# The borders of two layers in a two-layer attention and mixture-of-experts kernel: other orders on five engines, and key tiles with three maxima units in layer 0

## The reference: what is computed

```
x = x + L0_xattn(layernorm(x), ctx)      # 8 heads of 4
x = x + L0_ffn(layernorm(x))             # 8 experts, top 2, capacity 640
x = x + L1_xattn(layernorm(x), ctx)      # 16 heads of 16
x = x + L1_ffn(layernorm(x))             # 15 experts, top 3, and a shared one
# attention: softmax(q k^T * scale) v per head, then a projection with bias
```

## Time and profile before

| | us |
|---|---|
| median of 3 runs | 1242.67 |
| lowest, highest | 1241.54, 1252.23 |
| time of the profiled execution | 1248.94 |
| its span | 1247.2 |
| PE busy | 1107.5 (89%) |
| DVE busy | 751.6 (60%) |
| ACT busy | 527.8 (42%) |
| POOL busy | 474.8 (38%) |
| mean granted TensorE clock | 0.929 |

### The profile page before, as it was taken

How to read it: one execution, slowest core, us unless ns; L and a number is a source line. 1 busy time by engine, 2 the same in 40 slices (tenths; PEclk the granted TensorE clock), 3 DMA queues, 4 the chain that set the end, 5 groups by cost and what they waited for, 6 DMA issues and landing times. The chain is left out here.

```text
span 1247.2 us, 20458 instructions
## 1 busy us (share of the span) xinstructions
PE 1107.5 (89%) x6708; PEld 761.6 (61%) x6709; DVE 751.6 (60%) x1466; ACT 527.8 (42%) x1074; POOL 474.8 (38%) x518
## 2 busy tenths in 40 slices
PE   4788877699999999999658899998878999999997
PEld 1244444599999999999523444454545455555554
DVE  6878668367458557643467887876067244444427
ACT  4266653345336335522326666666324122323210
POOL 4203430556356546421335354102014066656510
PEclk9599987799999999999859999989568999999999
DMA  5122213533133123120343132320381422222242
GB/s 176 28 93 93 78 46 98 194 127 111 52 117 127 61 83 128 53 96 18 102 111 116 57 104 87 103 87 2 127 303 53 167 72 72 77 80 77 56 168 102
DMA packets 68048, 121.63 MB, mean 98 GB/s; under 512 B 16993, under 2 KB 36232, under 8 KB 67206
## 3 DMA queue, kind: packets, MB, share of 16 engines
q1 hardware_dynamic: 57894, 96.28, 23.6%
q0 software_dynamic: 10080, 24.38, 6.1%
HBM read 89.84 MB, written 33.82 MB: 99 GB/s over the span
## 5 line engine op out<-in xcount | busy, mean ns | idle before, releaser
L739 ACT ACTIVATE PT<-S 128x512 f32<-128x512 f32 x384 | 203.8, 599 | 124.3 <-PE S L717 123.3
L754 DVE TENSOR_REDUCE M<-S 128x2 f32<-128x1024 f32 x192 | 225.2, 1219 | 34.4 <-PE S L693 33.9
L510 PE MATMUL bankm<-XSTh,w12h 128*128 128x320 f32 x512 | 163.2, 319 | 5.3 <-DVE HF L594 5.2
L510 PE MATMUL bankm<-XSTl,w12h 128*128 128x320 f32 x512 | 159.7, 312 | 0.0
L510 PE MATMUL bankm<-XSTh,w12l 128*128 128x320 f32 x512 | 159.6, 312 | 0.0
L693 PE MATMUL S<-KS,QS 62*128 62x512 f32 x384 | 92.6, 498 | 43.2 <-DVE M L754 18.0
L588 DVE TENSOR_TENSOR HTl<-HF,HTh 128x320 fp32r<-128x320 f32 x128 | 129.7, 1013 | 1.0
L2199 PE MATMUL bank<-W,XST 128*128 x248 | 121.0, 610 | 4.6 <-issue 1.3
L717 PE MATMUL S<-QS,KS 64*128 64x512 f32 x384 | 112.0, 491 | 5.9 <-DMA QS<-NM 5.2
L727 PE MATMUL PV<-PT,VA 128*32 128x256 f32 x1536 | 109.6, 406 | 3.7 <-ACT PT L739 2.4
L554 ACT ACTIVATE SG<-bankm 128x320 f32<-128x320 f32 x128 | 56.1, 438 | 117.0 <-PE bankm L510 115.9
(11 more groups left out here) (274 smaller groups left out, 2008.6 us busy)
## 6 DMA issues: line engine op xcount, KB each, us to landing
stage<-in_W12T SPq DMA_DIRECT2D x32, 512.0 KB
stage<-in_W3T SPq DMA_DIRECT2D x16, 512.0 KB
W<-in_fc1T SPq DMA_DIRECT2D x2, 3840.0 KB, 18.8
YG<-yk SPq DMA_DIRECT2D x4, 1536.0 KB, 12.4
yk<-zeros SPq DMA_DIRECT2D x4, 1024.0 KB, 4.7
KS<-scrk SPq DMA_DIRECT2D x32, 128.0 KB, 2.7
scrq<-parts SPq DMA_DIRECT2D x16, 256.0 KB
QS<-scrq SPq DMA_DIRECT2D x30, 128.0 KB, 2.5
```

Of the source, the lines that this page charges most:

```text
L510: m = pe.matmul(bank[:, c % 2, 0:HALF], ew.w12[a][s][:, k, f:f + P], XST[b][:, k, half * HALF:(half + 1) * HALF], start=(k == 0 and (a, b) ...
L739: act.activation(self.PT[:, kt, 2 * j + h, :], self.S2[:, n % 3, :], ACT.Exp, scale=self.lay.scale).then_inc(self.exp_done, 1)
L754: dve.tensor_reduce(self.M[:, g % 2, :, h, q], got, AX.X, ALU.max).then_inc(self.ring.dve_free, 1)
```

## The change

Layer 0:
- FRONT0 falls from 14 to 10. The first scores come after unit (1,1), and key tiles 0 to 3 have three units each.
- DVE's `first_stats(3)` moves from ahead of `keep_values(1)` to behind the negation of group 0's maxima.

Layer 1:
- PE makes 11 value tiles ahead of the queries, and the other 5 between units (0,1) to (0,5). The bias products move behind the turn of group 0's maxima. XN of batch 1 is turned in key tile 2 instead of 0.
- ACT writes the ones of KS slots 0 and 1 after the eighth value copy, slot 2 after the twelfth, slot 3 after the last.
- DVE copies into QS ahead of the low part of query 1; the statistics of batch 1 move behind the negation of group 0's maxima.
- POOL clears QS slots 1 and 2 right after the ones in VA, and slot 3 after all value tiles.
- SP stores both queries ahead of the queries of group 1, and waits for slot 3's zeros and ones ahead of the loop.

```
-FRONT0, FRONT1 = AHEAD, UNITS + 2
+FRONT0, FRONT1, EARLY = UNITS + 2, UNITS + 2, 11
-TURN_XN, QUERY = {(0, 0): 1, (0, 15): 2, (1, 15): 3}, ...
+TURN_XN, QUERY = {(0, 2): 1, (0, 15): 2, (1, 15): 3}, ...
...
             low_keys(1)
-            first_stats(3)
             keep_values(1)
...
             at.negate(dve, 0)
+            first_stats(3)
...
+            at.load(sp, 1, "k")
+            store(0, 0)
+            store(0, 1)
+            sp.wait_ge(zeros_done, 1)
+            load(1, "q")
             sp.wait_ge(ones_done, 2)
-            at.load(sp, 1, "k")
-            sp.wait_ge(zeros_done, 1)
-            store(0, 0)
-            load(1, "q")
-            store(0, 1)
...
+            sp.wait_ge(zeros_done, 2)
+            sp.wait_ge(ones_done, 3)
             for g in range(NG):
...
+            pool.memset(at.QS[:, 1:SLOTS - 1, :, :].bitcast(F32), 0.0).then_inc(zeros_done, 1)
             pool.wait_ge(v_ready, NT)
-            pool.memset(at.QS[:, 1:, :, :].bitcast(F32), 0.0).then_inc(zeros_done, 1)
+            pool.memset(at.QS[:, SLOTS - 1, :, :].bitcast(F32), 0.0).then_inc(zeros_done, 1)
...
-            for t in range(NT):
+            for t in range(EARLY):
                 value(t)
...
-            pe.wait_ge(v_done, NT)
+            pe.wait_ge(v_done, EARLY)
...
             for u in range(UNITS):
                 at.maxima(pe, 0, u)
+                if 1 <= u <= NT - EARLY:
+                    value(EARLY + u - 1)
+            at.maxima(pe, 1, 0)
+            at.turn(pe, 0)
             pe.wait_ge(wo_loaded, 32)
...
-            at.maxima(pe, 1, 0)
-            at.turn(pe, 0)
...
-            for t in range(NT):
+            for t in range(EARLY):
                 keep_value(t)
-            fill_keys(slice(0, 1), 1)
+                if t == 2 * TPB - 1:
+                    fill_keys(slice(0, 2), 2)
...
-            fill_keys(slice(1, SLOTS), SLOTS - 1)
+            for t in range(EARLY, NT):
+                keep_value(t)
+                if t == 3 * TPB - 1:
+                    fill_keys(slice(2, 3), 1)
+            fill_keys(slice(3, 4), 1)
...
             low(0, 0)
-            low(0, 1)
             dve.wait_ge(at.picked, 2)
             dve.tensor_copy(at.QS[:, 0, 1, :], at.S2[:, 1, :]).then_inc(at.dve_stack, 1)
-            dve.wait_ge(added, 2 * PER)
-            link(norm_tiles(dve, pre, X, range(TPB, 2 * TPB)))
-            norm_seed(dve, link, pre, 1)
+            low(0, 1)
...
             at.negate(dve, 0)
+            dve.wait_ge(added, 2 * PER)
+            link(norm_tiles(dve, pre, X, range(TPB, 2 * TPB)))
+            norm_seed(dve, link, pre, 1)
```

More of the change, by code:

```diff
@@ L784 @@
 GPB1 = 16 // GH
-FRONT0, FRONT1 = AHEAD, UNITS + 2
+FRONT0, FRONT1, EARLY = UNITS + 2, UNITS + 2, 11
 TURN_OT, PROJECT, TURN_XF, ROUTE = 3, (4, 7), 11, 12
-TURN_XN, QUERY = {(0, 0): 1, (0, 15): 2, (1, 15): 3}, {(0, 3): (1, 0), (0, 4): (1, 1), (1, 0): (2, 0), (1, 8): (2, 1),
+TURN_XN, QUERY = {(0, 2): 1, (0, 15): 2, (1, 15): 3}, {(0, 3): (1, 0), (0, 4): (1, 1), (1, 0): (2, 0), (1, 8): (2, 1),
                                                        (2, 0): (3, 0), (2, 8): (3, 1)}
@@ L842, in ring0 @@
     names += [("max", 0, u) for u in range(UNITS)] + [("max", 1, 0), ("turn", 0)]
-    names += [("max", 1, u) for u in range(1, AHEAD - UNITS)]
+    names += [("max", 1, u) for u in range(1, FRONT0 - UNITS)]
     for g in range(NG):
```

## The result

| | before | changed |
|---|---|---|
| median of 20 runs, us | 1248.64 | 1242.09 |
| lowest, highest | 1239.84, 1254.34 | 1228.74, 1250.84 |
| ratio to before | | 0.9941, 95% interval 0.9917 to 0.9965 |
| profiled execution | 1248.94 | 1245.86 |

The change makes the kernel faster by 0.59% (0.35 to 0.83%), 7.4 us of 1248.64. The forecast was 12.2 us and 1230.5. So the forecast missed the changed kernel's median by 11.6: 6.0 in the starting point and 5.6 in the difference of the medians (6.55 instead of 12.2).

A forecast was written before the change was run, and what follows sets the result against it. The prediction took a single chain at each layer's start, up to the first scores, as the bound. Layer 1's -11.3 and layer 0's -0.9 made -12.2, from the median 1242.67 to 1230.5 us; range 1224.5 to 1239.5.

The forecast's parts named there:

- Steps 1 and 2: Layer 1 start: five value tiles leave the path, -4.3; KS fill moved, -0.4; POOL's clear of QS delays XN, +0.8.
- Step 3: Layer 1 start: copy into QS ahead of query 1's low part, batch 1 statistics moved, so reductions begin earlier; -2.65 us.
- Step 4: Layer 1 start: five value tiles between units make PE the bound there, +0.7 us, if the clock is 2.4 GHz.
- first rival: Layer 1's five value tiles between units run at 1.2 GHz: 5.9 us more than step 4, 1236.4; chance 12%.
- Steps 5 and 6: Layer 1 start: bias products run during NM's transfer, -2.0; NM's shift no longer waits in SP's queue, -2.95.
- Step 7: Layer 1 key tiles: XN's turn leaves key tile 0, -1.9, and goes to key tile 2 at 2.4 GHz; -0.5 net.
- the halving's wait: Layer 1, key tile 1: halving meets POOL's bias additions, longer by up to about 0.4 us; left out of the sum.
- third rival: Starts gain and key tiles give it back; layer 0 loses 2 to 4 us, or XN is late: 1236 to 1240; 11%.
- the case for a slower kernel: Clock fails to rise in layer 0's DVE-bound key tiles, each costing 2.07 us more at 1.2 GHz: 1255; chance 4%.

The follow-up runs named there:

- layer 1's part alone: Kernel before with only the layer 1 edits, FRONT0 and the place of the statistics as before; 1238.42 to 1243.33 before, ratio 0.9975.
- statistics in key tile 0: Changed kernel with FRONT0 back at 14 and layer 0's statistics of batch 3 moved into key tile 0; 1236.42 to 1243.33 before, ratio 0.9942.
- products at key tiles 17 to 20: Changed kernel with four unread 256-column products on PE, one at each of those key tiles of layer 0; 1236.54 to 1244.05 before, ratio 0.995.
- the later bias additions: Changed kernel with POOL's bias addition of layer 1's first two row tiles done one group later; 1237.46 to 1244.05 before, ratio 0.995.

## Why the prediction was wrong, step by step

The terms below are means over the profiles of kernels with the same code in the stage. Layer 1 as before: 4 profiles. Layer 1 as changed: 6 (both of the changed kernel, layer 1's part alone, statistics in key tile 0, products at key tiles 17 to 20, and the later bias additions, whose edit is worth at most 0.8 there). Layer 0 as before: 3. Layer 0 as changed: 7.

| | forecast | measured |
|---|---|---|
| L1, to first scores | -10.8 | 36.4 - 47.0 = -10.5 |
| L1, key tiles 0 to 3 | -0.5 | 22.5 - 21.3 = +1.2 |
| L1, all to the last exponential | -11.3 | 282.4 - 292.0 = -9.6 |
| L0, to first scores | -5.8 | 41.2 - 46.3 = -5.1 |
| L0, key tiles 0 to 3 | +4.95 | 23.5 - 17.3 = +6.2 |
| L0, all to the first value tile | -0.9 | 603.6 - 601.3 = +2.3 |
| sum | -12.2 | -7.3 |

The sum of the stages, -7.3, fits the -7.4 of the run times, closer than it had to. Single profiles of one code scatter by 7 us in the row of layer 1's whole attention and by 8 in that of layer 0, so the two wholes are good to some 3 us each. The rows to the first scores and of the key tiles scatter by 1 to 4. The scatter of layer 1's whole lies in its last eight key tiles: without them the gain is 10.0 where the row has 9.6.

*The number* is where it went most wrong: the step that failed is the last, "I carry the difference over to the median". With the median of the 20 runs, 1248.64, the same difference gives 1236.4. I noted that the profiled execution was 6.3 above the median of three, "with nothing in these stretches that would explain it". What explains it lay in stretches that I had not read. The second profile of the same kernel took 8.6 us less: 6.7 of them in the last eight key tiles of layer 1 (34.9 at a clock of 0.71 against 28.3 at 0.94) and 4.0 behind that attention, while it was 1.7 later at the start of layer 1 and 0.4 slower in the key tiles between.

Nor is 1248.64 the level of the kernel for good. Of the 20 runs six lie at 1239.8 to 1242.7 and fourteen at 1246.9 to 1254.3, with none between, and two of my three were of the lower lot. In the three other batches the kernel before has medians of 1243.33, 1244.05 and 1247.87, and its runs reach from 1237 to 1258. Over these 92 runs the time falls as the mean granted clock of the run rises (correlation -0.95, where -1 would be a straight line): what sets most runs apart is how long they are at 1.2 GHz, such as the stretch near 131 us (5.4 us), that in key tiles 2 and 3 of layer 0 (3.5), and that at the end of layer 1 (up to 6.7). The range, 1224.5 to 1239.5, had no part for it.

*Steps 1 and 2, value tiles and POOL's clear.* XNT came 4.4 earlier against a forecast of 3.9. PE came free at about 617.5 and XN was ready at 617.35: the clear's 1.73 us hit DVE as forecast, but PE would not have turned any earlier, so its price was 0.

*Step 3, DVE's order,* held: the reductions start at 626.12, 19.9 behind the first value tile instead of 27.1, -7.3 where the steps so far add up to -6.55.

*Step 4, value tiles between units,* is the term of the start that was mis-sized: +0.7 forecast, and in the first profile it took the lead from 7.3 at the first reduction to 4.4 at the halving, so it cost 2.9. My own condition was that the clock stay at 1.00. It fell for a moment (2.02 for the first tile, units of 0.79). Even at 2.4 GHz a unit and a tile follow each other every 1.49 (631.23 to 632.72) and not every 1.36. In one profile, that of the later bias additions, three of the units ran so and the scores came at 39.1, 3.2 later than the mean of the other five: about half of the first rival's 5.9.

*Steps 5 and 6* held: -5.1 together, forecast -4.95. From the halving to NM it is 1.43 instead of 3.61, and SP issues 0.3 behind NM's start instead of 3.2. The transfer takes 2.88 as before. So in the first profiles the start gained 9.5, 1.3 less than forecast: step 4 took 2.2 more, and the steps around it gave 0.9 more. In the means it gained 10.5.

*Step 7, key tiles,* was forecast at -0.5 and came out at +1.2 in the mean. The scatter allows a zero (three of the six profiles have 21.0 to 21.3, as before), but the parts are clear:

| key tile of layer 1 | forecast | measured |
|---|---|---|
| 0 | -1.9 | 3.5 - 5.6 = -2.1 |
| 1 | 0 | 7.3 - 5.7 = +1.6 |
| 2 | +1.4 | 6.1 - 4.3 = +1.8 |
| 3 | 0 | 5.7 - 5.7 = 0 |

The failed term is key tile 1, put at nothing. There the halving met POOL's additions, 1.34 instead of 0.17, of which key tile 1 gets back 0.7 to 0.8 when they are moved. It still takes 6.8 then, where the four profiles with layer 1 as before have 5.1 to 5.9; what makes up that rest no run shows. Key tile 2 holds for the mean, but not for the first profile: I took the turn of XN there at 2.4 GHz because the clock had risen there before, and it stood at 0.50 through key tiles 0 to 2. That is so in two of the six profiles, with 24.1 and 24.5 for the four tiles at a clock of 0.62 and 0.61; the three at 0.74 to 0.76 have 21.0 to 21.3, and with products to feed PE, at 0.96, they took 19.5.

By the Trainium skill (GPSIMD Engine Reference, Specifications) I had put the halving's wait at 0.4 at most and then left it out. The Trainium skill's SBUF — State Buffer, "SBUF: two separate sides", is nearer to the rows: it tells of a lock for a whole instruction that blocks the other engine fully. The cast began in the third of POOL's four additions and ended 0.03 us behind the last, so in this trace it waited for two of them and not for one. In layer 1's part alone it ended 0.03 behind the third, after 0.64, and the subtraction behind it took 0.65, to 0.03 behind the fourth.

*Layer 0.* The start gained 5.1 (forecast 5.8), and the four key tiles with three units gave back 6.2 (forecast 4.95), the largest part, 2.2, in key tile 1, so key tile 4 comes 1.1 later where I had it 0.9 earlier. My third rival, that a start gains and its key tiles give it back, is what happened, at a smaller price than I gave it. The remaining +1.2 lies where the code is equal and the clock isn't (the stretch near 131 us came in four of seven profiles with the changed layer 0, and in two of four with FRONT0 at 14 and no products at tiles 17 to 20). Whether the change makes it likelier is open.

The clock failing to rise for many key tiles, the case for a slower kernel, was not seen: in key tiles 0 to 3 of layer 0 the longest stretch at 0.50 was 15.8 us, in the profile with products at key tiles 17 to 20, and it ended:

```profile
41.90:57.70 15.80, 13.24 (x47) 4.89 (x47) 9.13 (x12) 6.23 (x12) 8.65 (x16) 0.50 0.09 28
```

## What to carry to other kernels

Take a kernel's level from many runs: where executions of one program spread over 1.5%, a median of three can be off by half a percent, nearly what the edit is worth. One profiled execution is no level either (two of the kernel before took 1248.94 and 1240.36). What can be forecast is the difference, with a range for the clock, and it is measured on runs of both kernels side by side. When a profile lies off the median, compare it with a second one stage by stage before the difference is carried over. A lead of maxima that is cut short at a start comes back as a longer key tile for each unit moved, so what pays is moving work that the start doesn't need (the statistics), and not starting with less in hand. And a stretch at 1.2 GHz doesn't keep its place in the program: what is moved next to a thinly fed stretch of PE should be priced at both levels of the clock.

## What the runs showed of the hardware

- The clock fell to 0.50 near 131 us of layer 0 although PE was busy 12.78 of 14.00 us there in a profile where it didn't fall. The same program had the fall in one execution and not in the next. With 16 us at 0.50 that stage took 5.4 us longer, less than half of the 16. The Trainium skill (TensorE: Matmul & The Clock Gate, A second HAM failure mode) tells of a kernel whose PE idles briefly between groups of products, often enough that its clock swings between its two levels. The rows fit that, with 1.22 us of short idle times in the 14.00; they don't show that it is the cause.
- The same eight key tiles at the end of layer 1's attention took 28.3 us at a mean clock of 0.94 and 34.9 at 0.71, in two executions of one program. Over 92 executions of it the time and the mean granted clock had a correlation of -0.95.
- A DVE cast of 16 elements took 1.34 and 1.29 us, and 0.18 alone, beside a run of POOL additions between tensors in SBUF, and ended 0.03 behind the last of them. A TENSOR_SCALAR of four elements took 1.73, to the end of a POOL memset, while DVE's reductions from PSUM beside the same POOL additions stayed at 1.22 each.
- From SP's issue of the 32x128 transfer of NM to the first scores, where nothing but it held them up, it was 2.75 to 2.91 us in every profile (2.88 in the timelines of both kernels).
